# A mixture-of-experts stage on one Trainium2 core: w2 and b2 read in place by register addresses, w1 copied one tile ahead

## What is computed

```python
h = jax.nn.relu(jnp.einsum('nd,edf->enf', xf, W1) + b1[:, None, :])
y = jnp.einsum('enf,efd->end', h, W2) + b2[:, None, :]
out = jnp.einsum('ne,end->nd', w, y)
```

## Time and profile before

| | us |
|---|---|
| median of 3 runs (420.7 to 424.39) | 421.6 |
| span of the profiled execution | 438.2 |
| tile stage, steady part of that execution (10 loop iterations, 60 tiles) | 281 to 395 |

### The profile page before, as it was taken

One profiled execution on the slowest core, in us unless ns is written; L12 is line 12 of the kernel. 1 busy time (PEld: TensorE's weight loads), 2 busy tenths in 40 slices (PEclk: granted clock), 3 DMA queues, 4 the chain that ended last, 5 costly groups with the idle time before them and its releaser, 6 DMA issues.

```text
span 438.2 us, 12358 instructions
## 1 busy us (share of the span) xinstructions
PE 363.8 (83%) x3127; PEld 321.2 (73%) x3127; DVE 313.1 (71%) x1170; ACT 253.5 (58%) x705; POOL 244.2 (56%) x566
## 2 busy tenths in 40 slices
PE   1679999999999999999996435999999999999300
PEld 1457888787787877878885313999999999999300
DVE  7666878788777887777974561777777777678154
ACT  1246677776667676676754101777777777677200
POOL 6111117776667767677677660466666665766500
PEclk9989999999999999999999556999999999999855
DMA  5355500001000000000000031222222222221198
GB/s 136 92 158 159 155 1 21 21 15 31 27 27 13 13 27 27 27 20 13 20 28 28 28 101 48 61 74 73 77 71 76 70 75 70 70 76 58 54 308 243
DMA packets 39227, 29.54 MB, mean 67 GB/s; under 512 B 4679, under 2 KB 35778, under 8 KB 39202
## 3 DMA queue, kind: packets, MB, share of 16 engines
q1 hardware_dynamic: 27858, 16.30, 13.6%
q0 software_dynamic: 4352, 9.45, 6.0%
q10 hardware_dynamic: 6992, 3.50, 2.8%
HBM read 16.50 MB, written 12.73 MB: 67 GB/s over the span
## 4 chain that ended last, share of the span: by engine, by line
PE 63%; DVE 14%; DMA 8%; issue 6%; SPq 5%; DVEq 1%; POOL 1%; ACT 1%; another core or an unknown queue 0%; POOLq 0%; ACTq 0%
PE ps_out L1320 7%; PE ps_oy L1332 7%; PE ps_vc L1332 7%; PE ps_q L1320 6%; PE ps_k L1175 5%; PE ps_out L1213 4%; DMA row_of<-ids_dram 4%; PE ps_oy L1228 4%; PE ps_vc L1175 3%; SPq L480 3%; PE ps_oy L1221 3%; PE ps_q L1175 3%; PE ps_vc L1203 3%; PE ps_ln L1312 2%; PE ps_k L1320 2%
## 5 line engine op out<-in xcount | busy, mean ns | idle before, releaser
L607 POOL DMA_INDIRECT y_dram<-heads_out,place x72 | 73.8, 1025 | 29.9 <-issue 25.9
L578 POOL DMA_INDIRECT slots_dram<-rows,row_id x64 | 63.3, 988 | 19.5 <-issue 19.5
L734 ACT ACTIVATE k_prime<-ps_q,b_T 128x128 f32<-128x128 f32 x108 | 31.8, 365 | 19.8 <-PE ps_q L1320 19.8
L734 ACT ACTIVATE k_prime<-ps_out,b_T 128x128 f32<-128x128 f32 x108 | 31.8, 366 | 19.0 <-PE ps_out L1320 18.9
L544 POOL TENSOR_TENSOR rstd<-moments,ln_eps 128x2 f32<-128x2 f32 x32 | 6.2, 195 | 62.3 <-DVE moments L821 62.1
L1332 PE MATMUL ps_oy<-w_tile,k_prime 128*128 128x128 f32 x288 | 38.1, 275 | 0.4 <-issue 0.4
L1332 PE MATMUL ps_vc<-w_tile,k_prime 128*128 128x128 f32 x288 | 38.1, 275 | 0.1
L1320 PE MATMUL ps_out<-sT,w_tile 128*128 128x128 f32 x288 | 38.1, 275 | 0.0
L539 POOL TENSOR_TENSOR spare<-minus_half,ln_eps 128x2 f32<-128x2 f32 x89 | 18.1, 204 | 35.1 <-ACT heads_out L743 22.1
L1213 PE MATMUL ps_out<-context,qT 128*128 128x130 f32 x256 | 36.1, 283 | 1.5 <-issue 0.8
L1091 DVE COPY w_tile<-w_all 128x640 f32 x72 | 36.0, 499 | 1.5
(11 more groups left out here) (232 smaller groups left out, 1028.2 us busy)
## 6 DMA issues: line engine op xcount, KB each, us to landing
qkv_rows<-slots_dram SPq DMA_DIRECT2D x72, 72.0 KB
w_all<-in_L_ffn_W SPq DMA_DIRECT2D x1, 2048.0 KB, 13.5
w_all<-in_L_ffn_W SPq DMA_DIRECT2D x8, 256.0 KB, 4.6
y_first<-y_dram SPq DMA_DIRECT2D x8, 256.0 KB, 5.6
y_second<-y_dram SPq DMA_DIRECT2D x8, 256.0 KB, 6.0
out<-y_first ACTq DMA_DIRECT2D x8, 256.0 KB, 5.5
y_dram<-heads_out,place POOLq DMA_INDIRECT x72
slots_dram<-rows,row_id POOLq DMA_INDIRECT x64
```

The costliest lines, as they stand in the source:

```text
L578: nc.gpsimd.indirect_dma_start(slots_dram[:, :], bass.IndirectOffsetOnAxis(row_id[:, place_of(p, a), j, k:k + 1], 0), rows[:, place_of(p, ...
L607: nc.gpsimd.indirect_dma_start(y_dram[:, :], bass.IndirectOffsetOnAxis(place[:, a, :], 0), y[:, a, :], None).then_inc(s_placed[a], 16)
L734: last = nc.scalar.activation(hT[:, a % 2, c, :], ps_up[a % 2][0][:, c * P:c * P + P], ACT.Relu, bias=b1_T[:, bass.ds(experts[0] * FC + c, ...
```

## The change

`w2_tile` and its semaphore go. TensorE takes the moving operand of the down product from `w2_all` itself, at an address that its sequencer computes from the expert of tile n - 1, and VectorE takes b2 of the same expert from there when it adds it to the down product. For that TensorE loads the word of experts too, at the head of each group. VectorE copies w1 for tile n + 1 instead of tile n + 2, as the first thing in its body instead of near its end. The digits of the word move by one tile, since the oldest expert now needed is that of tile n - 1; the digit numbers in the bodies of ScalarE and VectorE move along.

```diff
-            nc.vector.tensor_scalar(tile_expert[:, 0:FTILES], expert_f[:, :], float(E - 1), None, ALU.min)\
+            nc.vector.tensor_scalar(tile_expert[:, 1:1 + FTILES], expert_f[:, :], float(E - 1), None, ALU.min)\
...
             def slot_tile(n, a, i, experts):
+                if live(n + 1, FTILES):
+
+                    nc.vector.tensor_copy(w1_tile[:, (a + 1) % 3, :], w1_all[:, bass.ds(experts[2] * FF, FF)])\
+                        .then_inc(s_w1, 1)
                 if live(n, FTILES):
                     dve.wait_ge(s_up[1], n + 1)
                     wait(dve, s_down, n - 1)
...
-                if live(n + 1, FTILES):
-
-                    wait(dve, s_yb, n - 1)
-                    nc.vector.tensor_copy(w2_tile[:, (a + 1) % 3, :], w2_all[:, :, :].rearrange("p e d -> p (e d)")
-                                          [:, bass.ds(experts[1] * ((FC + 1) * D), (FC + 1) * D)]).then_inc(s_w2, 1)
-                if live(n + 2, FTILES):
-
-                    nc.vector.tensor_copy(w1_tile[:, (a + 2) % 3, :], w1_all[:, bass.ds(experts[2] * FF, FF)])\
-                        .then_inc(s_w1, 1)
                 if live(n - 1, FTILES):
                     dve.wait_ge(s_down, n)
                     wait(dve, s_yr, n - 2)
                     nc.vector.tensor_tensor(y_biased[:, (a - 1) % 2, :], ps_y[(a - 1) % 2][:, 0:D],
-                                            w2_tile[:, (a - 1) % 3, FC * D:], ALU.add).then_inc(s_yb, 1)
+                                            w2_flat[:, bass.ds(experts[0] * W2 + FC * D, D)],
+                                            ALU.add).then_inc(s_yb, 1)
...
-                    pe.wait_ge(s_w2, n)
                     wait(pe, s_yb, n - 2)
                     for c in range(FC):
-                        last = nc.tensor.matmul(ps_y[b][:, 0:D], hT[:, b, c, :], w2_tile[:, (a - 1) % 3, c * D:c * D + D],
+                        last = nc.tensor.matmul(ps_y[b][:, 0:D], hT[:, b, c, :],
+                                                w2_flat[:, bass.ds(experts[0] * W2 + c * D, D)],
                                                 start=(c == 0), stop=(c == FC - 1))
                     last.then_inc(s_down, 1)
 
-            slot_tiles(pe, slot_tile)
+            slot_tiles(pe, slot_tile, groups=group_experts)
```

More of the change, by code:

```diff
@@ L299, in lm_tower_kernel @@
         w1_tile = sb("w1_tile", [P, 3, FF])
-        w2_tile = sb("w2_tile", [P, 3, (FC + 1) * D])
+        w2_flat = w2_all[:, :, :].rearrange("p e d -> p (e d)")
+        W2 = (FC + 1) * D
         hT = k_prime[:, :, :].rearrange("p a (c t) -> p a c t", c=FC)
@@ L374, in lm_tower_kernel @@
         s_slots = [sem(f"rows_in_slots{a}") for a in range(2)]
-        s_w1, s_w2 = sem("w1_of_tile_ready"), sem("w2_of_tile_ready")
+        s_w1 = sem("w1_of_tile_ready")
         s_b1, s_b1r = sem("b1_transposed"), sem("b1_ready")
@@ L734, in slot_tile @@
                         last = nc.scalar.activation(hT[:, a % 2, c, :], ps_up[a % 2][0][:, c * P:c * P + P], ACT.Relu,
-                                                    bias=b1_T[:, bass.ds(experts[0] * FC + c, 1)])
+                                                    bias=b1_T[:, bass.ds(experts[1] * FC + c, 1)])
                     last.then_inc(s_hid[0], 1)
@@ L1080, in slot_tile @@
                         last = nc.vector.tensor_scalar(hT[:, a % 2, c, :], ps_up[a % 2][1][:, at:at + P],
-                                                       b1_T[:, bass.ds(experts[0] * FC + c, 1)], 0.0, ALU.add, ALU.max)
+                                                       b1_T[:, bass.ds(experts[1] * FC + c, 1)], 0.0, ALU.add, ALU.max)
                     last.then_inc(s_hid[1], 1)
@@ L1084, in slot_tile @@
                         dve.wait_ge(s_placed[a], 16 * i)
-                    nc.vector.tensor_copy(slot_w[:, a, :], slot_rows[:, a, bass.ds(experts[0] + D, 1)])
-                    nc.vector.tensor_copy(place[:, a, :], slot_rows[:, a, bass.ds(experts[0] + (D + E), 1)])\
+                    nc.vector.tensor_copy(slot_w[:, a, :], slot_rows[:, a, bass.ds(experts[1] + D, 1)])
+                    nc.vector.tensor_copy(place[:, a, :], slot_rows[:, a, bass.ds(experts[1] + (D + E), 1)])\
                         .then_inc(s_meta, 1)
-                if live(n + 1, FTILES):
-                    wait(dve, s_yb, n - 1)
-                    nc.vector.tensor_copy(w2_tile[:, (a + 1) % 3, :], w2_all[:, :, :].rearrange("p e d -> p (e d)")
-                                          [:, bass.ds(experts[1] * ((FC + 1) * D), (FC + 1) * D)]).then_inc(s_w2, 1)
-                if live(n + 2, FTILES):
-                    nc.vector.tensor_copy(w1_tile[:, (a + 2) % 3, :], w1_all[:, bass.ds(experts[2] * FF, FF)])\
-                        .then_inc(s_w1, 1)
                 if live(n - 1, FTILES):
```

## The result

Beside each other in four runs, the changed kernel takes 428.9 us (426.8 to 429.7) and the kernel before 421.3 us (420.7 to 424.4). The ratio is 1.013, with a 95% interval of 1.009 to 1.017: slower by 5.5 us, 3.7 to 7.3. The profiled execution of after has a span of 427.8 us. That is less than the 438.2 us of the profile of before, though the kernel is slower: the two profiles differ in the stages ahead of the tiles, which begin at 253 us in one and at 269 us in the other.

The account below looks back on a forecast made before the run. TensorE was taken to bound the tile loop at 1.90 us a tile. Nine loop heads at 0.38 us plus 0.1 at the entry made 3.5 us on the 421.6 us median: 425.1 us, range 421.4 to 430.0.

Parts of the forecast that it names:

- no fetch of code: At taken branches of TensorE's grown loop body: a rival had instruction fetches, 9 x 1.3 = 11.7 us, 433 us, chance 0.03.
- the dearer rival: TensorE's load or addressed matmuls cost more, 0.7 to 0.8 us a loop head, 7.3 us in all, 428.9 us; chance 0.22.
- The larger chance, 0.54: Chance that the measured time lies within about 1%, 4.2 us, of no change: 0.34 from the forecast plus the hidden case.
- The copies are worth nothing: VectorE loses the 128x640 w2 copy, 0.5 us a tile; TensorE did not wait for it, so booked at nothing.
- The addresses hide in an ordinary tile: Ahead of the first down matmul, three added instructions take 0.3 of 0.70 us spare, so an ordinary tile stays 1.90 us.
- 0.6 us for the addresses: On TensorE's sequencer, two register operations and four address instructions a tile, 6 x 0.1 = 0.6 us.
- 0.55 us for the load: TensorE's read of the experts' word at a loop head, with digit operation and range test: 0.55 us, taken from ScalarE.
- The restart: 0.07, mostly on the transpose: At a loop head, restarting TensorE after a stop costs 0.07 us more, most of it taken by the transpose.
- 0.38 a head: TensorE's stop at a loop head: transpose 0.27 us late, first up matmul 0.36 late, taken as 0.38 us; nine heads.
- w1 is 0.26 late at a head, covered: VectorE's w1 copy ends 0.26 us late for the next up matmuls, less than the 0.38 TensorE has already slipped.
- If TensorE's load were free, this would come out instead: Without TensorE's own slip at loop heads, the late w1 copy would set the price: 9 x 0.26 = 2.3 us.
- The entry, 0.1,: The loop's entry comes without decrement and branch, 0.3 us sooner than other heads, and keeps 0.1 us of cost.

Follow-up runs that it names:

- e8: Kernel before, but TensorE reads w2 of expert 0 in place at a fixed address and VectorE copies only b2, not w2: 423.2 us, ratio 1.001.
- e6: Changed kernel with TensorE's word load behind the iteration's first up product, w1 copied two tiles ahead and b2 copied by itself: 422.8 us, ratio 1.0000.
- e9: e5 with VectorE also copying b2, so its addition reads a fixed address; w1 still one tile ahead: 443.4 us, ratio 1.006 to the kernel before.
- e7: Changed kernel with TensorE's load of the experts' word done twice at each loop head: 435.0 us, ratio 1.029 to the kernel before.
- e4: Changed kernel, load and addresses kept on TensorE, but w1 copied two tiles ahead and b2 copied by itself: 454.7 us, ratio 1.012 to the kernel before.
- e1: Kernel before, with TensorE also loading the experts' word at each group's head without using it: 449.5 us, ratio 1.0015.
- e2: Changed kernel without TensorE's load, the expert in its addresses counted from the group's number: 456.2 us, ratio 1.015 to the kernel before.
- e5: Changed kernel with TensorE's word load moved behind the up matmuls, ahead of the waits for hidden values: 428.2 us, ratio 1.015 to the kernel before.
- e3: Kernel before with only the w1 copy moved, one tile ahead and first in VectorE's body; w2 still copied: 448.9 us, ratio 0.9998.
- e10: e5 with three long-satisfied waits ahead of VectorE's w1 copy at a loop head: 448.0 us, ratio 1.017 to the kernel before.

## Why the prediction was right, and which terms were off

The direction, the mechanism and the place of the stops came out: nine heads, a stop ahead of the transpose that is no semaphore's, ordinary tiles at 1.896 us, no gain from the copies, and no fetch of code (11 packets in the queue of the earlier trace rows, as before, and no packet of either instruction queue between 283.2 and 389 us of the profile of after, where eight of the nine heads lie). The time, 428.9 us, is not the 425.1 of the forecast but that of the dearer rival, 3.8 us more, and inside the range. That it is the rival's figure to the digit is luck. The rival had 0.75 us a head, from a load dearer by 0.4 us or addresses dearer by 0.08 each, and 0.5 at the entry. The load was dearer by 0.15 and all six operations together by 0.09, a head cost 0.67, and the stage grew by 6.4 us and not by 7.3. The larger chance, 0.54, had stood on a change within 1%; it was 1.3%, for which 0.42 had been left. Step by step:

- *The copies are worth nothing.* Right by e8. That "VectorE's busy time falls by 30 us in 60 tiles" was wrong: 0.24 us a tile, 14 us in 60. The records of the copies, 29.9 us, did go.
- *The addresses hide in an ordinary tile.* Right: 1.896 us with them in e6, e9 and after.
- *0.6 us for the addresses.* They took 2 x 0.096 + 4 x 0.124 = 0.69.
- *0.55 us for the load.* It took 0.70. The rows chosen were ScalarE's, and the record of the load is about as short on TensorE (303 ns, the median of 12); but the gaps behind each record are longer there. e7 shows 0.65 for a second one by itself.
- *The restart: 0.07, mostly on the transpose.* This was the third miss. The lateness of the up matmul isn't the transpose's plus a trifle: it came as 0.39 ahead of the transpose and 0.21 more behind it. The sequencer has waits to pass between the two and now no lead to do it in.
- *0.38 a head.* It was 0.60 without w1. Addresses, load and line 1307 add 0.69 + 0.70 + 0.10 = 1.49 us to the sequencer. The runs agree on the lead that hides it: 1.49 - 0.60 = 0.89 us (e4), and the 0.75 us of e1 hide. The prediction had 1.25 - 0.36 = 0.89 too. The lead was read rightly, and the whole miss is in what was laid on it: 0.60 in place of 0.38, 2 us over nine heads.
- *w1 is 0.26 late at a head, covered.* It was 0.67 late alone (e2) and 0.54 beyond the late load's own 0.13 (e5), so the cover left 0.07 a head uncovered. By the trace of e2, VectorE's load starts 0.91 us behind the last pass of the down product, where the prediction had 0.82 (305.9 against 305.08). Load and digits take 0.66 in place of 0.60, the two register operations with the address 0.37 in place of 0.25, and the copy 0.67 in place of 0.43. That is 0.51 more; with 0.07 in place of 0.15 for TensorE's sequencer to pass the wait, 0.26 becomes 0.69. Against e9, the copy in e5 starts 0.31 us later (0.20 us ahead of the next transpose and not 0.52) and takes 0.25 us longer: 0.56, measured 0.54. Of the 0.31 only 0.07 is shown to be the addition's address operation; what slows the register operations behind it is open.
- *"If TensorE's load were free, this would come out instead"*: right as a mechanism, at 9 x 0.67 and not 9 x 0.26.
- *The entry, 0.1,* cost 0.40: it comes without a branch, but the load and the addresses stand there too.
- *The end: nothing.* 0.12 us in the last tiles, off the chain.

Nine heads of 0.67 and the entry make 6.4 us; the ratio gives 5.5 us, 3.7 to 7.3. The 3.5 of the forecast lies outside by a little. The floor of 600 ns that the Trainium skill has for a tensor_load ("DMA: Bandwidth & Descriptors", section "Latency and other measured facts") would have given 6.5 us, near the measured. The trace doesn't bear it out as the load's duration, 303 ns, but as a price of the whole block on TensorE, 0.70 us, it is nearer than what I took from ScalarE.

## What to carry to other kernels

An edit that puts register work into the sequencer of the engine that sets the time costs nothing until it exceeds the sequencer's lead at the worst place, a loop head, and all of it beyond. Price it by that engine's own distances between starts, not by another engine's records. When two engines become late at one place, undoing either shows nothing: e5 alone would have acquitted the load. And a copy taken away from an engine with spare time buys nothing, while the register address that replaces it can delay what stands behind.

## What the runs showed of the hardware

**GpSimd's indirect DMA holds up a VectorE copy that starts in a certain part of it.** In seven kernels (after, e2, e3, e5, e7, e9, e10), 323 w1 copies of 128x512 by their start behind that of an indirect transfer (those more than 1.2 us behind one and more than 0.5 us ahead of the next are left out), in the trace's starts and durations:

| starts behind it, us | copies | took, us | ended behind it, us |
|---|---|---|---|
| -0.49 to -0.14 | 66 | 0.42 to 0.45 | up to 0.27 |
| -0.10 to 0.03 | 27 | 0.42 to 0.50 | 0.33 to 0.46 |
| 0.05 to 0.48 | 34 | 0.43 | 0.48 to 0.91 |
| 0.53 to 0.57 | 32 | 0.68 down to 0.64 | 1.21 |
| 0.61 to 0.70 | 12 | 0.60 down to 0.51 | 1.21 |
| 0.77 to 1.19 | 152 | 0.42 to 0.44 | 1.21 to 1.62 |

A copy that starts between 0.53 and 0.77 us ends at 1.21 whenever it starts, as if its 0.43 us began at 0.78. The transfer's record is 0.98 us. The Trainium skill has a rule for it: "SBUF — State Buffer", section "SBUF: two separate sides", calls the port pair that the two engines share an exclusive lock: whichever of the two starts first gets it for its whole instruction, and the other is blocked. A hold of that kind is seen here; "for the whole instruction" is not: copies that start 0.05 to 0.48 us into the transfer's record run at full speed, and only starts in a quarter of a microsecond within it are held. Nor is every start in it: one 128x512 copy in before and one in e1, which start 0.54 and 0.53 us behind their transfers, take 0.42 us. The records of those two transfers are 1.07 us long and not 0.98. That the lock is what holds the copy is argued from the common end at 1.21; no run takes the transfer away.

**A register address moves the wait.** With it, the wait for the down product stands on an address operation of the sequencer, and the addition starts 0.44 us behind the start of the last down pass. Where the addition waits for it by itself the least is 0.31 us (e3, e4, e6, e8), and 0.37 in e9, where a wait instruction stands ahead. And the sequencer gets no further meanwhile: VectorE's load at a head starts 0.01 us behind the addition in before, 0.48 behind it in after.

**Open.** In several profiles, that of before among them, TensorE has a longer stop at the 57th tile, and in e1 and e4 more of them in the tiles behind it. It was not looked for by an experiment. In the trace of before:

```profile
375.60 0.89 ACT L734 ACTIVATE k_prime<-ps_q,b_T 128x128 f32<-128x128 f32 x3 [1.30 <-PE ps_q L1320]
...
376.40 0.35 DVE L1080 TENSOR_SCALAR k_prime<-ps_k,b_T 128x128 f32<-128x128 f32 x1 [2.09 <-PE ps_k L1320]
```

The 1.30 and 2.09 us are how long ScalarE and VectorE stood idle, though the up products that they wanted were by the records long done; TensorE then waited for the hidden values. By the trace their sequencers started nothing for 1.3 us (from 374.04) and 1.4 us (from 374.68). It is no fetch of code: no packet of an instruction queue moved between 316 and 399 us. The stop is 0.7 us in before and 2.1 in e2. It is absent in after and in e5 to e8, and it comes in the profiles with the longer early stages (before, e1 to e4, e9, e10). The lengths above leave it out.
